# A value projection by seven quarter products per pair of blocks, with running sums kept in PSUM

## The chip, the cores and the metric

One core of one Trainium2 chip runs the kernel. The metric is the device time of one execution in microseconds; lower is better. The core's engines are TensorE (PE; its weight loads are shown apart as PEld), VectorE (DVE), ScalarE (ACT), GpSimd (POOL) and SyncE (SP), which here only issues DMAs. Matmuls write to PSUM, which has 8 banks of 128 x 512 f32; GpSimd's instructions here never touch it.

## What is computed

A transformer layer over 4096 rows of 512: attention with a window of 64, a residual and layer norm, then a gated feed-forward with int8 weights, a residual and layer norm.

```python
qkv = x @ w_qkv.T                      # 4096 x 512 by 512 x 1536, 16 heads of 32
q = q * cos + _rotate_half(q) * sin    # the same for k
scores = jnp.einsum('bhqd,bhkd->bhqk', q, k) * scale
keep = (rel >= 0) & (rel < window)     # window is 64
attn = jax.nn.softmax(jnp.where(keep[None, None], scores, -jnp.inf), axis=-1)
out = jnp.einsum('bhqk,bhkd->bhqd', attn, v) ... @ w_out.T
x = _layernorm(x + out)
gate = jax.nn.silu(_qmatmul(x, w_gate, s_gate))
up = _qmatmul(x, w_up, s_up)
x = _layernorm(x + _qmatmul(gate * up, w_down, s_down))
```

## The kernel before

The rows are cut into 8 tiles (0 to 7) of 512, a tile into 4 blocks of 128. One pass of the loop (`body`) does the attention of tile a and the feed-forward of tile f = a - 1. Each engine has its own instruction list, written out by hand; a `wait` stands before the instruction that needs it and holds up everything behind it on that engine. There is no scheduler.

On PE a pass runs: the value projection of a and its first score steps; 16 steps, each with one gate group (8 matmuls onto bank 0 or 2) and one up group (bank 1 or 3) of f, and between them the score steps and `weigh_v` (probabilities by values) of a; the output projection of a as two pairs (`project_o_pair`); the down projection of f; then q and k of tile a + 1 as two pairs (`project_pair`). A pair is two blocks, 2i and 2i + 1.

The projections of q and k and the output projection already used seven products for eight (Winograd's form): the input's four quarters (front, back block by low, high half of the 512 columns) and the weight's four quarters are combined into sums, and seven quarter products of two matmuls each give what eight would. Before, each product had a place of its own in PSUM and DVE added them up: `sum_second`, `sum_fourth`, `sum_back_odd` and four more for q and k, `sum_o_second` and eight more for the output. ACT copied only the first product (`keep_first`, `keep_o_first`). x's sums (`x_sums`) are made on DVE by `sum_x` (tile 1's second pair on POOL, by `sum_second_x`). The value projection was plain: `project_v`, four blocks of four 512-column matmuls, V0 at the end of the pass before, V1, V2, scores 0 and 1, V3. `keep_v` (ACT) rounded a block from its bank to f16 in `v_own`, and `split_v` (DVE) stored what rounding left.

After the q and k products: `rope_products` (DVE) reads the banks, `rope_sums` makes the rotated values in `fuse`, `split_high(j)` (ACT, four copies) and `split_low(j)` (POOL, four subtractions) split block j into two f16 parts, and SP transposes them (`turn_qk`, two DMAs a block, released by `qk_low`) into `qkT`. Blocks j and j + 2 share a buffer (`qk_split[j % 2]`), so `split_high(2)` and `split_high(3)` wait until the transposes of blocks 0 and 1 have landed (`wait_qkT`). In tile 0's pass SP issues half-size transposes (`first_turn_qk`).

Each tile's sums for the output projection overwrite columns 0 to 1023 of `wg` and 0 to 511 of `wu`; POOL loads them anew (`reload_columns`). In the first pass (`first`) PE projects q and k of tile 1, pair 1 last, ACT runs `split_x1_high(0..3)`, the split of the layer's middle rows, and DVE `split_x1`, `finish_x1`, then `rope_front(1)`.

## Time and profile before

| what | us |
| --- | --- |
| median of three runs (1166.36 to 1168.07) | 1166.68 |
| the profiled execution, first to last instruction | 1164.2 |
| PE busy | 1154.0 |
| DVE busy | 984.6 |
| ACT busy | 584.4 |
| POOL busy | 587.3 |

The profile is of one execution. An engine's busy time is no bound by itself; PE's share of the chain that ended last, and whether its groups follow each other without a hole, tell whether it bounds the kernel. The granted clock of PE is at its full level in all 40 slices but is shown only in tenths (9 is 90% or more). A 512-column f32 matmul stands as two entries in a timeline's count, so a quarter product of two matmuls is "x4". A row's duration includes the tail in which the next one already runs; distances between starts are what a group costs.

### The profile page before, as it was taken

The numbers are of one execution on the slowest core, as the hardware profiler recorded it, in microseconds if no ns is written. First come the engines' busy times: TensorE is split into PE (matmuls) and PEld (weight loads), VectorE is DVE, ScalarE is ACT, GpSimd is POOL, SyncE is SP. The second block draws the span as 40 slices with busy tenths as digits, with TensorE's granted clock in tenths as the row PEclk, the third lists the DMA queues.
The fourth block names the chain that finished last, engine by engine and source line by source line (L and its number), as shares of the span: only waits on it lengthen the run. The fifth ranks groups of instructions, "written<-read, shape, count | busy, mean of one in ns | idle before, by whom it ended". The sixth has DMA issues, their size and how long they took to land.

```text
span 1164.2 us, 25539 instructions
## 1 busy us (share of the span) xinstructions
PE 1154.0 (99%) x8433; PEld 567.9 (49%) x8433; DVE 984.6 (85%) x2821; ACT 584.4 (50%) x1640; POOL 587.3 (50%) x563
## 2 busy tenths in 40 slices
PE   9999999999999999999999999999999999999998
PEld 4344446444464444644455444554445444464444
DVE  7899998898987899879998899897898988986434
ACT  3953883048820588105880169701686027950330
POOL 0775684156731667326771367613676236752330
PEclk9999999999999999999999999999999999999999
DMA  9999786366562765617656096561964537734000
GB/s 295 173 175 252 137 166 160 66 88 137 111 149 55 110 131 107 145 41 128 132 97 141 37 146 119 101 132 46 155 123 88 131 63 137 120 73 109 19 2 36
DMA packets 352077, 134.80 MB, mean 116 GB/s; under 512 B 309840, under 2 KB 332496, under 8 KB 351952
## 3 DMA queue, kind: packets, MB, share of 16 engines
q1 hardware_dynamic: 334976, 106.86, 49.6%
q0 software_dynamic: 10560, 17.30, 5.1%
q10 hardware_dynamic: 6416, 9.00, 2.1%
q8 instruction: 75, 1.23, 0.5%
q14 instruction: 50, 0.41, 0.1%
HBM read 32.19 MB, written 8.39 MB: 35 GB/s over the span
## 4 chain that ended last, share of the span: by engine, by line
PE 97%; DVE 1%; ACT 1%; issue 1%; POOL 0%; POOLq 0%; DVEq 0%
PE bank L842 61%; PE bank L1058 18%; PE bank L848 10%; PE bank L984 3%; PE bank L964 2%; PE bank L864 1%; PE bank L1080 1%; ACT bank L1243 1%; PE bank L873 0%; PE bank L1069 0%; PE bank L948 0%; DVE wd L1373 0%; ACT wu L1186 0%; DVE ffn_tmp L1530 0%; ACT fuse L1186 0%
## 5 line engine op out<-in xcount | busy, mean ns | idle before, releaser
L842 PE MATMUL bank<-x1T,wg 128*128 128x512 f16 (+1 forms) x1032 | 242.5, 378 | 0.0
L842 PE MATMUL bank<-x1T,wu 128*128 128x512 f16 x1024 | 241.9, 379 | 0.0
L1243 ACT ACTIVATE bank<-bank,neg_max,qk_scale 128x128 f32<-128x128 f32 x512 | 220.5, 435 | 7.8 <-DVE neg_max L1558 6.1
L1058 PE MATMUL bank<-wd,fuse 128*128 128x512 f16 (+2 forms) x1056 | 222.7, 373 | 0.0
L660 POOL TENSOR_TENSOR fuse<-ffn_tmp,fuse 128x512 f16<-128x512 f32 x128 | 149.7, 1170 | 117.5 <-ACT fuse L1186 116.8
L742 POOL TENSOR_TENSOR fuse<-fuse 128x512 f16<-128x512 f32 x116 | 137.7, 1218 | 74.9 <-ACT fuse L1186 72.8
L1058 PEld LDWEIGHTS bank<-wd,fuse 128*128 128x128 f16 x1056 | 101.9, 98 | 118.0
L842 PEld LDWEIGHTS bank<-x1T,wu 128*128 128x128 f16 x1024 | 100.1, 98 | 120.7
L655 POOL TENSOR_TENSOR xT_sb<-probs,xT_sb 128x512 f16<-128x512 f32 x112 | 129.6, 1158 | 44.5 <-ACT xT_sb L1186 44.4
L842 PEld LDWEIGHTS bank<-x1T,wg 128*128 128x128 f16 x1032 | 96.3, 98 | 113.9 <-issue 4.0
L1196 ACT ACTIVATE ffn_tmp<-bank,tanh_scale 128x512 f32<-128x512 f32 x128 | 88.2, 689 | 100.0 <-PE bank L842 76.8
L848 PE MATMUL bank<-wqkv,xT_sb 128*128 128x512 f32 x296 | 133.6, 599 | 0.0
L1552 DVE CUSTOM_DVE_ANT_0 bank<-bank,mask_tile 128x128 f32<-128x128 f32 x448 | 116.3, 321 | 0.0
L1569 DVE SCALAR_TENSOR_TENSOR ffn_tmp<-bank,fuse_scale,ffn_tmp 128x512 f32<-128x512 f32 x128 | 96.1, 751 | 20.8 <-PE bank L842 9.9
L1565 DVE SCALAR_TENSOR_TENSOR ffn_tmp<-ffn_tmp,bank 128x512 f32<-128x512 f32 x128 | 86.9, 679 | 27.3 <-ACT ffn_tmp L1196 27.3
L1243 ACT ACTIVATION_READ_ACCUMULATOR bank<-bank,neg_max,qk_scale 128x1 f32 x512 | 107.0, 209 | 0.0
L823 POOL TENSOR_TENSOR rstd<-mean_var,half_power 128x1 f32<-128x1 f32 x32 | 23.8, 745 | 149.7 <-DVE mean_var L1586 144.2
L1186 ACT ACTIVATE fuse<-fuse 128x512 f16<-128x512 f32 x120 | 65.5, 618 | 55.0 <-DVE fuse L1381 54.5
L1530 DVE SCALAR_TENSOR_TENSOR probs<-bank,inv_sum 128x512 f32<-128x512 f32 x120 | 82.9, 691 | 4.8 <-DVE inv_sum L1525 0.3
L848 PEld LDWEIGHTS bank<-wqkv,xT_sb 128*128 128x128 f32 x296 | 54.7, 190 | 63.4 <-issue 61.7
L1186 ACT ACTIVATE fuse<-ffn_tmp 128x512 f16<-128x512 f32 x128 | 79.5, 621 | 8.2 <-DVE ffn_tmp L1569 8.2
L1373 DVE TENSOR_TENSOR fuse<-bank,tables 128x512 f32<-128x512 f32 x120 | 75.4, 680 | 1.5 <-ACT fuse L1186 1.0
(235 smaller groups left out, 1621.5 us busy)
## 6 DMA issues: line engine op xcount, KB each, us to landing
v_cross<-v_own SPq DMA_DIRECT2D x64, 128.0 KB, 2.4
out<-x ACTq DMA_DIRECT2D x31, 256.0 KB, 2.0
xT_sb<-xT SPq DMA_DIRECT2D x30, 256.0 KB, 4.1
qkT<-x SPq DMA_DIRECT2D x28, 256.0 KB, 3.8
wg<-w_gate POOLq DMA_DIRECT2D x7, 1024.0 KB, 5.2
wu<-w_up POOLq DMA_DIRECT2D x7, 512.0 KB, 6.0
wqkv<-w_qkvT SPq DMA_DIRECT2D x8, 256.0 KB, 6.3
wg<-w_gate POOLq DMA_DIRECT2D x1, 2048.0 KB, 8.4
```

The source lines that it names most:

```text
L655: done(probs_low, pool.tensor_tensor(place[:, 1, :, :], probs_place(s, ffn), place[:, 0, :, :], ALU.subtract))
L660: done(fuse_low, pool.tensor_tensor(fuse[:, s, 1, :], ffn_tmp[:, s % 2, :], fuse[:, s, 0, :], ALU.subtract))
L742: last = pool.tensor_tensor(*low_operands(j, i, ffn), ALU.subtract)
L842: last = pe.matmul(dst, lhsT, rhs, start=(i == 0), stop=(i == len(pairs) - 1))
L848: last = pe.matmul(dst, xT_sb[:, j, k, :], wqkv[:, k, cols], start=(k == 0), stop=(k == KC - 1))
L1058: last = pe.matmul(dst[:, cols], fuse[:, s, z, rows], wd[:, s, cols], start=(s == 0 and z == 0), stop=(s == STEPS - 1 and z == 1))
L1186: return act.activation(dst, src, ACT.Copy, scale=scale)
L1196: done(tanh_done, act.activation(ffn_tmp[:, s % 2, :], bank32[2 * (s % 2)], ACT.Tanh, scale=tanh_scale[:, s:s + 1]))
L1243: last = act.activation(unit, unit, ACT.Exp, bias=neg_max[:, s % 2, h // 3, h % 3:h % 3 + 1], scale=qk_scale[:, 2:3], accum_out=row_sum[:, ...
L1552: last = dve.tensor_tensor_reduce(out=unit, in0=unit, in1=mask_tile[:, :], scale=1.0, scalar=MASKED, op0=ALU.add, op1=ALU.max, accum_out=r ...
L1565: done(gated, dve.scalar_tensor_tensor(out=tmp, in0=tmp, scalar=1.0, in1=bank32[2 * (s % 2)], op0=ALU.add, op1=ALU.mult))
L1569: done(fused, dve.scalar_tensor_tensor(out=tmp, in0=bank32[2 * (s % 2) + 1], scalar=fuse_scale[:, s:s + 1], in1=tmp, op0=ALU.mult, op1=ALU ...
```

## The change

The value projection of tiles 1 to 7 becomes `project_values`: seven quarter products for each of the pairs 0 and 1, of two 256-column matmuls. The value weight's sums are made by POOL (`add_v_weights`, three per tile, and `lessen_v_weights` once) in the columns of `wu` above 1023, which POOL loads anew each tile, as those of `wg` (`reload_late_columns`, at step 2).

All three projections now keep running sums in PSUM. A product is added onto what the bank holds (`onto=True`), and where an intermediate sum is itself a result part, ACT first copies it to SBUF (`keep_fifth`, `keep_sixth`, `keep_seventh`, `keep_o_...`, `keep_values_...`), mostly to `late_rows`, the columns of `wg` above 1023 seen as f32. DVE adds two terms where it added up to four: three sums a pair for q and k, four row additions a pair for the output, one `add_v` a block for v. `keep_v` and `split_v` now read `late_rows` instead of a bank.

PE, value stage and its waits:

```diff
+            def quarter(dst, lhsT, rhs, onto=False):
+                return product(dst, [(lhsT[:, k, :], rhs[:, k, :]) for k in range(KC // 2)], onto)
...
+            def values_first(a, i):
+                front_low, front_high, back_low, back_high = x_quarters(i)
+                low_left, right_less_left, high_left, high_right = v_quarters()
+                wait(rope_read, pe, a, i)
+                done(v_product[i], quarter(v_places(i)[3], front_low, low_left))
+
+            def values_fifth(a, i):
+                low_left, right_less_left, high_left, high_right = v_quarters()
+                wait(x_summed, pe, a - 1, 7)
+                wait(v_weights_added, pe, a - 1, 2)
+                done(v_product[i], quarter(v_places(i)[1], x_sums(i)[:, 0, :, :], right_less_left))
...
+            def values_sixth(a, i):
+                wait(v_products_kept[i], pe, a - 1, 0)
+                done(v_product[i], quarter(v_places(i)[3], x_sums(i)[:, 1, :, :], added_v_weights(0), True))
...
+            def values_seventh(a, i):
+                wait(v_products_kept[i], pe, a - 1, 2)
+                done(v_product[i], quarter(v_places(i)[3], x_sums(i)[:, 2, :, :], added_v_weights(1), True))
...
+            def values_fourth(a, i):
+                front_low, front_high, back_low, back_high = x_quarters(i)
+                wait(v_products_kept[i], pe, a - 1, 3)
+                done(v_product[i], quarter(v_places(i)[2], back_high, added_v_weights(2)))
+
+            def project_values(a):
+                values_first(a, 0)
+                values_fifth(a, 0)
+                values_first(a, 1)
+                values_sixth(a, 0)
+                values_third(a, 0)
+                values_fifth(a, 1)
+                values_seventh(a, 0)
+                values_sixth(a, 1)
+                values_second(a, 0)
+                values_fourth(a, 0)
+                values_third(a, 1)
+                values_seventh(a, 1)
+                scores(a, 0, True)
+                scores(a, 1, True)
+                values_second(a, 1)
+                values_fourth(a, 1)
...
                     elif attn:
-                        wait(v_low, pe, a, 2 * s + 1)
+                        wait(v_added, pe, a - 1, 2 * s + 1)
```

PE, output projection of a pair (the third product is now the sixth):

```diff
+                done(o_product, quarter(chain, front_low, low_left))
                 wait(added, pe, a - 1, 1 - i)
-                if i == 0:
-                    wait(probs_ready, pe, a, STEPS - 1)
-                else:
-                    wait_o_sum(pe, a, 0, SUM_THIRD)
                 wait(out_weights_added, pe, a - 1, 3)
-                done(o_product, quarter(back_right, added_o(i, 2), added_out(2)))
-                wait(o_first_kept, pe, a - 1, i)
-                done(o_product, quarter(front_left, front_high, high_left))
+                done(o_product, quarter(other, added_o(i, 2), added_out(2)))
                 wait(added, pe, a - 1, 2)
-                if i:
-                    wait_o_sum(pe, a, 0, SUM_BACK_LEFT)
-                done(o_product, quarter(back_left, added_o(i, 1), added_out(1)))
-                done(o_product, quarter(front_right, added_o(i, 0), added_out(0)))
-                wait_o_sum(pe, a, i, SUM_SECOND)
-                done(o_product, quarter(back_left, back_high, added_out(3)))
+                wait(o_products_kept, pe, a - 1, 4 * i)
+                done(o_product, quarter(chain, added_o(i, 1), added_out(1), True))
+                wait(o_products_kept, pe, a - 1, 4 * i + 1)
```

ACT, in the loop and in the first pass:

```diff
+            def keep_values_first(a, i):
+                if i == 0:
+                    wait(pair_summed, act, a - 1, 3 * turn_of(1) + 2)
+                keep_value_product(a, i, late_rows(2 * i)[:, 0:HALF_EMB], v_places(i)[3], V_FIRST)
...
                 split_high(a + 1, 0, True)
+                keep_first(a + 1, 1)
                 for j in range(2):
                     split_x1_high(a, j, ffn)
                 split_high(a + 1, 1, True)
-                keep_first(a + 1, 1)
+                keep_fifth(a + 1, 1)
+                keep_sixth(a + 1, 1)
+                keep_seventh(a + 1, 1)
                 carry_v(a + 1)
...
+                    keep_values_first(a, 0)
+                    keep_values_fifth(a, 0)
+                    keep_values_first(a, 1)
+                    keep_values_sixth(a, 0)
+                    split_high(a, 2, ffn)
+                    keep_values_fifth(a, 1)
+                    keep_values_seventh(a, 0)
+                    keep_values_sixth(a, 1)
+                    split_high(a, 3, ffn)
                     keep_v(a, 0, ffn)
-                    split_high(a, 2, ffn)
                     keep_v(a, 1, ffn)
+                    keep_values_seventh(a, 1)
+                    exponentials(a, 0, ffn)
                     keep_v(a, 2, ffn)
-                    split_high(a, 3, ffn)
-                    exponentials(a, 0, ffn)
                     keep_v(a, NB - 1, ffn)
                     exponentials(a, 1, ffn)
...
+                    keep_seventh(a + 1, 0)
                     keep_first(a + 1, 1)
                     split_high(a + 1, 0, ffn)
+                    keep_fifth(a + 1, 1)
+                    keep_sixth(a + 1, 1)
+                    split_high(a + 1, 1, ffn)
+                    keep_seventh(a + 1, 1)
                     carry_v(a + 1)
```

DVE and POOL:

```diff
+            def add_v(a, j):
+                i, back = j // 2, j % 2
+                wait(v_products_kept[i], dve, a - 1, 2 + back)
+                wait(v_product[i], dve, a - 1, V_FOURTH if back else V_SECOND)
+                done(v_added, dve.scalar_tensor_tensor(out=late_rows(j), in0=bank32[j], scalar=v_scale[:, 1:2],
+                                                       in1=late_rows(j), op0=ALU.mult, op1=ALU.add))
...
+                    add_v(a, 0)
+                    add_v(a, 1)
                     for j in range(2):
                         split_v(a, j, ffn)
                     for s in range(2):
                         maxima(a, s, ffn)
                         bias(a, s)
+                    add_v(a, 2)
+                    add_v(a, 3)
+                    weights(a, 0, ffn)
                     split_v(a, 2, ffn)
-                    weights(a, 0, ffn)
                     split_v(a, NB - 1, ffn)
                     weights(a, 1, ffn)
...
             def rope_front(a, i):
-                sum_front_even(a, i)
-                wait(pair_summed, dve, a - 1, 7 * turn_of(i) + 4)
+                add_front_even(a, i)
+                wait(pair_summed, dve, a - 1, 3 * turn_of(i))
                 rope_products(a, 2 * i, True, range(2), paired=True)
-                sum_front_odd(a, i)
-                if i:
-                    sum_back_even(a, i)
-                wait(pair_summed, dve, a - 1, 7 * turn_of(i) + 5)
+                add_back_odd(a, i)
+                add_front_odd(a, i)
+                wait(pair_summed, dve, a - 1, 3 * turn_of(i) + 2)
                 rope_products(a, 2 * i, True, range(2, 4), paired=True)
                 rope_sums(a, 2 * i, True)
...
+                sum_first_x(0)
                 split_low(a + 1, 0, True, range(2))
                 invert_deviation1(a, 2)
                 split_low(a + 1, 0, True, range(2, 4))
+                lessen_v_weights()
+                add_v_weights(a + 1, None)
                 for j in range(2):
                     keep_x1(a, j, ffn)
...
+                    if s == 2:
+                        reload_late_columns(a, f, attn)
```

How the lists of instructions change at the three places that matter.

ACT at the head of the loop's pass, before. `v_own<-bank` is `keep_v`, the two rows `fuse<-fuse` together are `split_high` of one block (2, then 3), `bank,row_sum` are the exponentials:

```order
L1186 ACTIVATE v_own<-bank0,v_scale 128x16x32
L1186 ACTIVATE fuse<-fuse 128x16x2x16 x2
L1186 ACTIVATE fuse<-fuse 128x32x16 x2
L1186 ACTIVATE v_own<-bank1,v_scale 128x16x32
L1186 ACTIVATE v_own<-bank2,v_scale 128x16x32
L1186 ACTIVATE fuse<-fuse 128x16x2x16 x2
L1186 ACTIVATE fuse<-fuse 128x32x16 x2
L1243 ACTIVATE bank4,row_sum<-bank4,neg_max,qk_scale 128x128 x4
L1186 ACTIVATE v_own<-bank3,v_scale 128x16x32
```

The same place in the changed kernel; `wg<-bank` are the copies of value sums to `late_rows`:

```order
L1285 ACTIVATE wg<-bank1,v_scale 128x256
L1285 ACTIVATE fuse<-fuse 128x16x2x16 x2
L1285 ACTIVATE fuse<-fuse 128x32x16 x2
L1285 ACTIVATE wg<-bank2,v_scale 128x256
L1285 ACTIVATE wg<-bank1,v_scale 128x256
L1285 ACTIVATE wg<-bank3,v_scale 128x256
L1285 ACTIVATE fuse<-fuse 128x16x2x16 x2
L1285 ACTIVATE fuse<-fuse 128x32x16 x2
L1285 ACTIVATE v_own<-wg 128x16x32 x2
L1285 ACTIVATE wg<-bank3,v_scale 128x256
L1384 ACTIVATE bank4,row_sum<-bank4,neg_max,qk_scale 128x128 x4
```

Four copies now stand behind `split_high(2)`, and the last of them, of bank 3, also behind `split_high(3)` and two `keep_v`.

PE at the end of the value stage, before (V1, V2, scores 0 and 1, V3, first gate group):

```order
L848 MATMUL bank1<-wqkv,xT_sb 128x512 x4
L848 MATMUL bank2<-wqkv,xT_sb 128x512 x4
L964 MATMUL bank4<-qkT 32x96 x16
L964 MATMUL bank6<-qkT 32x96 x16
L848 MATMUL bank3<-wqkv,xT_sb 128x512 x4
L842 MATMUL bank0<-x1T,wg 128x512 x8
```

The same place in the changed kernel, from seventh(0) on:

```order
L876 MATMUL bank1<-wu,ffn_tmp 128x256 x2
L876 MATMUL bank3<-wu,probs 128x256 x2
L876 MATMUL bank0<-wqkv,xT_sb 128x256 x2
L876 MATMUL bank1<-wu,xT_sb 128x256 x2
L876 MATMUL bank2<-wqkv,probs 128x256 x2
L876 MATMUL bank3<-wu,probs 128x256 x2
L1063 MATMUL bank4<-qkT 32x96 x16
L1063 MATMUL bank6<-qkT 32x96 x16
L876 MATMUL bank2<-wqkv,xT_sb 128x256 x2
L876 MATMUL bank3<-wu,xT_sb 128x256 x2
L876 MATMUL bank0<-x1T,wg 128x512 x8
```

The last value product goes to bank 3, whose other half holds the sum that ACT must have copied.

ACT at the end of the first pass, before; `qkT<-x1` are the `split_x1_high`, `y<-bank4` the copy of the first product of pair 1, `v_cross<-v_cross` is `carry_v`:

```order
L1186 ACTIVATE qkT<-x1 128x512 x2
L1186 ACTIVATE fuse<-fuse 128x16x2x16 x2
L1186 ACTIVATE fuse<-fuse 128x32x16 x2
L1186 ACTIVATE y<-bank4 128x512
L1186 ACTIVATE v_cross<-v_cross,carry_scale 64x1024
L1186 ACTIVATE qkT<-x1 128x512 x2
```

And in the changed kernel:

```order
L1285 ACTIVATE qkT<-x1 128x512 x2
L1285 ACTIVATE fuse<-fuse 128x16x2x16 x2
L1285 ACTIVATE fuse<-fuse 128x32x16 x2
L1285 ACTIVATE wg<-bank7 128x512
L1285 ACTIVATE wg<-bank6 128x512 x2
L1285 ACTIVATE v_cross<-v_cross,carry_scale 64x1024
L1285 ACTIVATE qkT<-x1 128x512 x2
```

The last two `split_x1_high` now stand behind three copies of product sums.

## Rows read from the trace of the kernel before

**Rows 1.** Page: the span, and part 4, the chain by engine.
```profile
span 1164.2 us, 25539 instructions
...
PE 97%; DVE 1%; ACT 1%; issue 1%; POOL 0%; POOLq 0%; DVEq 0%
```

**Rows 2.** Timeline of PE, one tile: start us, us, engine, line, operation, names, count.
```profile
507.95 1.88 PE L842 MATMUL bank<-wqkv,xT_sb 128*128 128x512 f32 x4
...
531.98 10.46 PE L848 MATMUL bank<-wqkv,xT_sb 128*128 128x512 f32 x24
...
542.37 0.52 PE L964 MATMUL bank<-qkT 128*32 128x96 f16 x32
...
542.83 3.70 PE L848 MATMUL bank<-wqkv,xT_sb 128*128 128x512 f32 x8
...
546.36 1.89 PE L842 MATMUL bank<-x1T,wg 128*128 128x512 f16 x8
...
550.20 1.90 PE L842 MATMUL bank<-x1T,wg 128*128 128x512 f16 x8
```

**Rows 3.** Timeline of ACT, same tile; in brackets idle time before and releaser.
```profile
468.34 0.38 ACT L1186 ACTIVATE ffn_tmp<-bank 128x256 f32<-128x256 f32 x1 [0.20 <-PE bank L842]
...
522.37 2.18 ACT L1186 ACTIVATE fuse<-fuse 128x512 f16<-128x512 f32 x4
...
536.51 2.19 ACT L1186 ACTIVATE fuse<-fuse 128x512 f16<-128x512 f32 x4 [0.21 <-DMA qkT<-fuse]
```

**Rows 4.** Timeline of SP's DMA issues, and us to landing from the DMA view.
```profile
527.69 20.87 SPq L511 DMA_TRANSPOSE qkT<-fuse  x6
...
538.25 2.02 SPq L511 DMA_TRANSPOSE qkT<-fuse  x1
...
qkT<-fuse SPq DMA_TRANSPOSE x1, 4.3
...
24.59 11.94 SPq L521 DMA_TRANSPOSE qkT<-fuse  x8
...
35.19 1.34 SPq L521 DMA_TRANSPOSE qkT<-fuse  x1
...
qkT<-fuse SPq DMA_TRANSPOSE x1, 3.2
```

**Rows 5.** DVE and POOL, same tile; L1380 by source: ns min, median, max.
```profile
L1380 DVE TENSOR_TENSOR fuse<-fuse x29: 678/693/1455, 19.6 to 964.7; 128x512 f32<-128x512 f32 x29
...
539.97 1.64 DVE L1381 TENSOR_TENSOR fuse<-fuse 128x512 f32<-128x512 f32 x1
...
542.86 0.29 DVE L1552 CUSTOM_DVE_ANT_0 bank<-bank,mask_tile 128x128 f32<-128x128 f32 x1
...
545.43 0.74 DVE L1518 SCALAR_TENSOR_TENSOR v_own<-bank,v_scale,v_own 128x512 f16<-128x512 f32 x1
...
523.07 4.51 POOL L742 TENSOR_TENSOR fuse<-fuse 128x512 f16<-128x512 f32 x4 [4.74 <-ACT fuse L1186]
...
537.22 5.41 POOL L742 TENSOR_TENSOR fuse<-fuse 128x512 f16<-128x512 f32 x4 [1.98 <-ACT fuse L1186]
```

**Rows 6.** Timeline of PE and DVE in the output projection of pair 1.
```profile
475.80 1.03 PE L842 MATMUL bank<-wout,v_own 128*128 128x256 f32 x4
...
476.66 1.89 PE L842 MATMUL bank<-wg,x1T 128*128 128x256 f32 x8
...
476.02 0.42 DVE L1452 TENSOR_TENSOR x1T<-x1T,v_own 128x256 f32<-128x256 f32 x1
```

**Rows 7.** Timeline of tile 1: ACT, DVE, PE.
```profile
101.71 1.14 ACT L1186 ACTIVATE v_cross<-v_cross,carry_scale 64x1024 f16<-64x1024 f16 x1
...
102.75 0.62 ACT L1186 ACTIVATE qkT<-x 128x512 f16<-128x512 f32 x1
...
107.71 1.29 DVE L1373 TENSOR_TENSOR fuse<-bank,tables 128x512 f32<-128x512 f32 x2
...
120.59 1.89 PE L842 MATMUL bank<-x1T,wg 128*128 128x512 f16 x8
```

440 lines of the change are left out of this document (234 added, 206 removed).

## The prediction

> **What bounds the kernel now.** I read the page first, then the PE timeline of one tile in the middle of the loop, then what ACT, DVE, POOL and the DMA queue do beside it. The page puts 97% of the chain that ended last on PE [rows 1]. In the timeline the groups of matmuls start without a hole [rows 2], so every column that PE is spared is worth its time, and every wait put in front of PE costs its time. The tile that I use begins with the first product of pair 0 at 507.95; I call that T and count from it. The value projection starts at T+24.03 (531.98), is broken by the 32 matmuls of two score steps at T+34.42, and the first gate group starts at T+38.41 (546.36) [rows 2]. That is 14.38 us, of which the scores take 0.46 us, so the projection takes 13.92 us.
>
> **The saving.** A 256-column quarter product takes 0.86 us (475.80 to 476.66) [rows 6]. The new projection is 14 of them: 12.04 us. It spares 1.88 us a tile, 13.2 us over seven tiles. Without a new wait the execution of 1164.2 us would end near 1151. The rest of the text asks how much of this comes back as waits.
>
> **The value stage, tiles 2 to 7.** The order on PE is: first(0), fifth(0), first(1), sixth(0), third(0), fifth(1), seventh(0), sixth(1), second(0), fourth(0), third(1), seventh(1), scores, second(1), fourth(1). Products onto a running sum wait until ACT has copied the sum. A 256-column copy takes 0.38 us [rows 3], and there is always at least one other quarter, 0.86 us, in between, so copies alone would stall nobody. (A 512-column quarter of q and k takes 24.03 / 14 = 1.72 us [rows 2].) But ACT has split_high(2) and split_high(3) between them, 2.19 us each [rows 3], and these wait for the transposes of q and k of blocks 0 and 1, because two blocks share one buffer. fourth(1), PE's last value product, waits for the copy of seventh(1), which stands on ACT behind split_high(3) and behind two keep_v copies. Before, split_high(3) stood behind only what PE had already left. So the question is when block 1's transposes land.
>
> Upstream of it: split_high(0) starts at T+14.4 as before (522.37) [rows 3], because keep_first(1) waits for a product that ends at T+13.9 in both kernels. POOL's split_low(0) follows at T+15.1 and took 4.51 us alone, but 5.41 us beside DVE sums of two SBUF operands, which themselves then took up to 1.45 and 1.64 us, for a median of 0.69 [rows 5]. DVE now reaches rope_sums(1) some 5 us earlier, while split_low(0) runs, so I take 5.4: T+20.5 instead of T+19.7 (527.69, the first transpose) [rows 4]. split_high(1) now runs at about T+19.1, and split_low(1) is done at about T+25, so block 1's transposes stand right behind block 0's.
>
> Block 0's took 8.8 us (527.69 until ACT is let go at 536.51) [rows 3, 4]. What two blocks take back to back tile 0 shows: eight half transposes issued from 24.59, the last at 35.19, landing 3.2 us later [rows 4]; 13.8 us for both. (An issue alone takes 1.34 us there, so some of this may be SP's time and not the transfer's; full-size ones need half as many.) So block 1 lands at T+20.5+13.8 = T+34.3; with 19.7 it is T+33.5; if transposes overlap better than in tile 0, T+31 to T+32. Before, block 1's last transpose was issued at 538.25 and landed 4.3 us later, T+34.6 [rows 4]. It is issued 3 us earlier than before and lands hardly earlier, since the queue is what takes the time.
>
> From there: split_high(3) 2.1 (four copies pipelined), keep_v(0) and keep_v(1) 0.5 each, the copy 0.4, with semaphores 3.6 us. fourth(1) starts at T+37.9 and the first gate group at T+38.8, against T+38.4. PE would have wanted fourth(1) at T+24.0 + 13 x 0.86 + 0.5 = T+35.8. **The 1.88 us come back whole, and 0.4 on top.**
>
> **The second gate group.** It writes banks 2 and 3 and so waits for add_v(3). On DVE that stands behind split_v(0), split_v(1), the maxima and biases of steps 0 and 1 and add_v(2). PE comes to it 3.84 us after the first (546.36 to 550.20) [rows 2]. The maxima took 2.57 us for two steps (542.86 to 545.43) [rows 5]. split_v(0) can start 2.7 us after split_high(3) starts, at T+37.0. The two split_v now read two SBUF operands each while POOL runs split_low(3); by the lengthened sums [rows 5] I take 1.2 each (pipelined), 0.6 if they don't meet POOL. Then 37.0 + 2.4 + 2.6 + 1.4 = T+43.4 against T+42.6: 0.85 us of stall; with 0.6 each none. The Trainium skill ("SBUF — State Buffer", Who interferes with whom) says that a DVE instruction with two SBUF inputs contends with a GpSimd instruction that reads SBUF, and one with a single SBUF input does not. By that rule the new split_v pays what the sums paid, and the old one, whose first operand was in PSUM, did not; no row shows a split_v with both in SBUF.
>
> **The output projection, all seven tiles.** DVE goes from 18 instructions a tile to 8, ACT from two copies to eight. By the same slots (quarter 0.86, copy 0.38) each copy is there 0.2 to 0.3 us before PE wants it. One edge is new: the third product of pair 1 now is the sixth product and needs add_back_o(2). PE wants it where its third product started, 475.80; that sum started at 476.02 and ended at 476.44 [rows 6], and DVE comes to it about 0.35 us earlier than before. Cost 0.1 to 0.3 us less a small wait that goes; I take 0.15. The q and k pairs go from 7 DVE sums to 3 and from one ACT copy to four each; a slot is 1.72 us for a copy of about 0.6, and split_high(1), done at T+21.3, leaves the last copy (T+21.9) before its product (T+22.3). I find no stall; 0.4 us is the cover, and what passes it costs as much. (That DVE is the first to be late here if it slips: rope_done(1) lets split_high(1) go.) POOL's three weight sums, at split_low's 1.1 us or a little more each, fall into its idle time during the down projection; the reload of 2 MB of gate and up columns is issued at gate step 2 and needed at step 8, six steps of 3.5 us or more. Both at nothing, unless DMA contention counts (below).
>
> **Tile 1.** Here ACT's new order costs once. split_x1_high(2) ran at 102.75, then rope products of pair 1 started at 107.71 [rows 7]. Now split_x1_high(2) and (3) stand behind keep_seventh(1) and carry_v. PE's order up to there: second(1) early, first(1) at 92.9, project_o(3), then fifth, sixth, third, seventh, with about 0.4 us of waiting; seventh ends near 105.5. Copy 0.6, carry_v 1.14 [rows 7], so split_x1_high(2) ends at 107.8; split_x1(2), finish_x1(3), split_x1_high(3), split_x1(3) on DVE and ACT follow each other to 110.4, and pair 1's rope starts then, 3.4 us late. late_rows are free for the first value copy only after add_front_odd(1), near 114.1. PE wants sixth(0) at 107.9 + 2.6 = 110.5 and gets it at 114.5: 4 us. POOL's keep_x1(3) and split_low(1) also come 3.6 us later, block 1 lands near 121, rope_done(3) comes near 122, fourth(1) near 125.6, the first gate near 126.4 against 120.59 [rows 7]: 5.8 us lost. Bounds: 4 us (only the wait before sixth(0), less the 1.9 spared, plus the waits of the stage) to 7.
>
> **The sum.** Tiles 2 to 7: 0.4 + 0.85 + 0.15 = 1.4, six times 8.4. Tile 1: 5.8 + 0.85 + 0.15 = 6.8. Together +15 us: a span of 1179, and since the median of the runs lies 2.5 us above this execution's span, 1181.5 us. Bounds of the same story: no stall at the second gate and block 1 a little earlier (0.1 a tile) with 5 in tile 1 gives 1172; block 1 at T+35 and 7 in tile 1 gives 1187.
>
> **Rivals.** *Even in the loop.* Split_low(0) isn't lengthened, block 1 lands at T+33.5, no stall at the second gate: first gate at T+38.0, so -0.4 + 0.15 a tile, -1.5 in six; tile 1 +4.5: 1169.7. For it: part of tile 0's 13.8 us may be issuing, and DVE had slack before. 18%.
>
> *Faster.* Block 1's transposes land about 7 us after they are issued, whatever is before them, as block 1's last did within 4.3 us when the queue was empty: T+31 to T+32.2 [rows 4]. Then ACT reaches split_high(3) at T+31.9, the copy of seventh(1) is there at T+35.5 and PE never waits. The whole 1.88 less 0.15 holds: -10.4 in six tiles, +4 in tile 1: 1160.5. It decides at T+32.2: a landing before it brings all, each us after it costs one. Against it: eight half transposes took 13.8 us, not 9 [rows 4]. The Trainium skill ("Advanced Engine Details and Errata", X-Bar Transpose) expects 350 to 400 GB/s of transposes; a block is 1 MB, so by that page two blocks would take some 6 us and the rival would hold with room. The 13.8 us are 150 GB/s; here row and rule differ, and I go by the row. If tile 1 also recovered, 1155. 22%.
>
> *More stalls in the attention loop.* Everything after the second gate is 3 us nearer to PE: probabilities are split later on POOL, and the 2 MB reload is issued exactly when transposes of steps 2 and 3 run. If these land 1 to 2 us late, weigh_v waits 1 us a tile: 1189. 12%.
>
> *It doesn't do what it says:* 256-column products cost more than half of 512-column ones. The 0.86 us against 1.72 [rows 2, 6] speak against it; 1%, not priced.
>
> The forecast itself has the remaining 47%.
>
> **How the numbers follow.** A measurement of this kernel can tell about 0.2% (2.3 us) from no change. Faster: the faster rival, 22%. Same: half of the even rival, 9%. Slower: the rest, 69%. The range leaves out a tile 1 that recovers in the faster rival and the far end of the stalls: 1160 to 1189.
>
> **What would show it.** In the changed trace: the last value group of PE starts 37 to 38 us after T, with a hole of 1 to 2 us before it, let go by ACT wg; ACT's fuse copies before it are let go by DMA qkT. A hole of some 4 us at tile 1's fourth value product. The second gate group waits for DVE's wg. If instead the gate starts 36.7 us after T, the transposes were early and the faster rival holds. If the chain shows PE waiting at its half-bank copies in the output projection, my slots are wrong.

## The result: 1212.1 us, 3.9% slower

| | before | changed kernel |
|---|---|---|
| time, median of the runs | 1166.5 us (1166.2 to 1168.1) | 1212.1 us (1210.3 to 1213.7) |
| span of the profiled execution | 1164.2 us | 1208.9 us |
| mean granted clock of TensorE | 1.000 | 0.991 |

The ratio is 1.0386, with a 95% interval of 1.0367 to 1.0404. The forecast was 1181.5 us with a range of 1160 to 1189, so the time lies 23 us above the range's upper end.

The page of the changed kernel: its span, the chain that ended last by engine, and two of the DMA queues (packets, MB, share of 16 engines).

```profile
span 1208.9 us, 25954 instructions
...
q0 software_dynamic: 19008, 31.98, 9.3%
...
q8 instruction: 81, 1.33, 0.4%
...
PE 55%; issue 16%; POOL 11%; DVE 8%; DMA 6%; ACT 3%; SPq 1%; POOLq 0%; DVEq 0%; ACTq 0%
```

Before, PE had 97% of that chain and "issue" 1% [rows 1]. Now PE has 55%, and 16% is "issue", time in which an engine waited for nothing that the profile shows. PE no longer bounds the kernel by itself, but the 16% are not one cause: in the run below whose holes are gone they are still 13%, and in one with five such holes they are 2%. The stages tell more.

In PE's timeline I took the start of each stage and summed over the program; the last 33.4 us, from the last down projection on, are the same in both. The differences add up to the 44.7 us of span:

| stage | before | changed | difference |
|---|---|---|---|
| up to the first gate group of tile 1 | 120.6 | 129.5 | +8.9 |
| value stage, tiles 2 to 7 | 86.3 | 83.5 | -2.8 |
| feed-forward stages | 494.4 | 512.4 | +18.0 |
| output projection | 91.5 | 95.2 | +3.7 |
| down projection, all but the last | 193.7 | 193.7 | 0.0 |
| start of q and k to start of the value stage, tiles 2 to 7 | 144.2 | 161.1 | +16.9 |

**Of the 16.9 us, 16.5 are five holes of 3.2 to 3.4 us**, one at the start of the value stage of tiles 2 to 6 (measured from start to start; the idle time in a row's brackets is some 0.2 us less). Tile 7's value stage, and tile 1's, have none. Tiles 2 to 6 are those that TensorE reaches over a taken branch of its loop: the first pass and the last two are written out, and the loop is entered by falling into it. PE (first) and ACT around one of them, start us, us, engine, line, operation, names, count, and in brackets the idle time before and its releaser:

```profile
557.81 1.94 PE L876 MATMUL bank<-w_sums,xT_sb 128*128 128x512 f32 x4
562.82 2.07 PE L876 MATMUL bank<-wqkv,xT_sb 128*128 128x256 f32 x4 [3.06 <-issue]
564.68 1.62 PE L876 MATMUL bank<-wqkv,ffn_tmp 128*128 128x256 f32 x4
```
```profile
555.04 2.19 ACT L1285 ACTIVATE fuse<-fuse 128x512 f16<-128x512 f32 x4 [1.59 <-DVE fuse L1546]
557.14 0.57 ACT L1285 ACTIVATE wg<-bank 128x512 f32<-128x512 f32 x1
```

The row at 557.81 is `pair_fourth(1)`, the last product of the pass. It waits for the copy of the seventh product, ACT's row at 557.14, which ends at 557.71. The first product of the next pass starts 5.11 us after that; the same distance is 5.31, 5.27, 5.08 and 5.15 us in the other four passes. Only the 1.7 us of `pair_fourth(1)` lie over it.

**Behind the hole TensorE's clock falls.** The quarters at 562.82 and 564.68 take 1.86 and 1.46 us instead of 0.86. The windows of these stretches, with the busy time of each engine and then PEclk, DMA share and GB/s:

```profile
core 0: us, PE busy (x) PEld busy (x) DVE busy (x) ACT busy (x) POOL busy (x), PEclk, DMA share, GB/s
562.80:564.60 1.80, 1.78 (x4) 1.52 (x5) 1.76 (x4) 0.00 (x0) 0.00 (x0) 0.50 1.79 179
564.60:566.10 1.50, 1.50 (x5) 1.19 (x4) 1.22 (x2) 0.47 (x1) 0.00 (x0) 0.57 0.47 102
566.10:568.00 1.90, 1.90 (x10) 1.67 (x10) 0.00 (x0) 0.95 (x2) 0.00 (x0) 1.00 1.26 275
707.30:710.40 3.10, 0.15 (x1) 0.00 (x0) 3.06 (x6) 0.00 (x0) 1.35 (x2) 1.00 1.47 120
710.50:712.30 1.80, 1.80 (x8) 1.61 (x9) 1.77 (x4) 0.47 (x1) 0.00 (x0) 1.00 1.77 213
```

A granted clock of 0.50 is the lower of the two levels, 1.2 instead of 2.4 GHz. The last two rows are the next pass: a hole of 3.0 us, and no fall. Over the tiles the value stage takes 14.3, 14.5, 14.3, 12.8, 14.5 and 12.9 us, so four of the five holes brought the fall, at 1.5 to 1.7 us each. The clean stage, 12.84 us against 14.38 before, is the change's real saving, 1.54 us a tile.

**The feed-forward stages** lose 18.0 us, mostly in `weigh_v`, which waits for transposes of probabilities. PE at steps 0 to 3, and SP's issues of these transposes:

```profile
593.10 0.29 PE L1083 MATMUL bank<-xT_sb,v_cross 128*32 128x128 f16 x8 [0.69 <-DMA xT_sb<-xT_sb]
...
601.35 0.30 PE L1083 MATMUL bank<-y,v_cross 128*32 128x128 f16 x8 [0.49 <-DMA y<-xT_sb]
...
602.16 0.29 PE L1083 MATMUL bank<-y,v_cross 128*32 128x128 f16 x8 [0.40 <-DMA y<-xT_sb]
```
```profile
585.70 1.23 SPq L553 DMA_TRANSPOSE xT_sb<-xT_sb  x1
...
593.95 6.18 SPq L553 DMA_TRANSPOSE y<-xT_sb  x2
```

The first transpose is issued 8.6 us after the first gate group (577.15 to 585.70); before it was 5.5 us (546.36 to 551.82). In the DMA view the transposes to y take 6.0 us to land, against 3.1 before, in the stretch in which the 2 MB of late columns come in.

### The profile page after: what moved, and what is told of

Its sections match the earlier page's. It is cut to its first block, busy times and chain, and to the rows that moved or that the text cites. A ratio compares the mean times of both kernels' runs of the same rounds, so it can differ in the third digit from the quotient of the medians.

```text
span 1208.9 us, 25954 instructions
## 1 busy us (share of the span) xinstructions
PE 1159.1 (96%) x8601; PEld 606.4 (50%) x8601; DVE 977.0 (81%) x2727; ACT 641.1 (53%) x1777; POOL 645.0 (53%) x605
## 4 chain that ended last, share of the span: by engine, by line
PE 55%; issue 16%; POOL 11%; DVE 8%; DMA 6%; ACT 3%; SPq 1%; POOLq 0%; DVEq 0%; ACTq 0%
PE bank L876 34%; PE bank L1148 18%; POOL fuse L768 7%; DMA y<-xT_sb 4%; POOL xT_sb L656 2%; PE bank L1083 2%; ACT bank L1384 1%; DVE fuse L1538 1%; POOL fuse L661 1%; DVE qkT L1601 1%; PE bank L1063 1%; DMA out<-x 1%; DMA xT_sb<-xT 1%; ACT fuse L1285 1%; PE bank L902 1%
## 5 line engine op out<-in xcount | busy, mean ns | idle before, releaser
L768 POOL TENSOR_TENSOR fuse<-fuse 128x512 f16<-128x512 f32 x116 | 147.4, 1304 | 91.4 <-ACT fuse L1285 88.3
L656 POOL TENSOR_TENSOR xT_sb<-probs,xT_sb 128x512 f16<-128x512 f32 x112 | 129.9, 1160 | 79.4 <-ACT xT_sb L1285 79.2
L876 PEld LDWEIGHTS bank<-x1T,wu 128*128 128x128 f16 x1024 | 100.2, 98 | 120.6
L876 PE MATMUL bank<-wqkv,xT_sb 128*128 128x256 f32 (+1 forms) x216 | 84.1, 515 | 17.6 <-issue 15.7
L1285 ACT ACTIVATE fuse<-bank 128x512 f32<-128x512 f32 x24 | 14.3, 597 | 153.3 <-PE bank L876 153.3
L1285 ACT ACTIVATE wg<-bank 128x256 f32<-128x256 f32 (+1 forms) x84 | 37.9, 451 | 99.9 <-PE bank L876 99.9
```

Of the source, the lines that this page charges most:

```text
L656: done(probs_low, pool.tensor_tensor(place[:, 1, :, :], probs_place(s, ffn), place[:, 0, :, :], ALU.subtract))
L768: last = pool.tensor_tensor(*low_operands(j, i, ffn), ALU.subtract)
L876: last = pe.matmul(dst, lhsT, rhs, start=(i == 0 and not onto), stop=(i == len(pairs) - 1), skip_group_check=onto)
L1285: return act.activation(dst, src, ACT.Copy, scale=scale)
```

## Experiments on the loop's branch

In what follows theory A says that a taken branch of TensorE's loop costs a fixed way from the release of the last wait before it to the first product behind it, about 5 us, and that only work queued behind that wait covers it. Its rivals are an operand of the new products that comes late, and the longer program.

### Three quarters, or one, ahead of the branch

The comments behind `#` in the cuts of code are this text's.

```
-                values_first(a, 0)          # head of project_values(a), behind the branch
-                values_fifth(a, 0)
-                values_first(a, 1)
...
+                    values_first(a + 1, 0)  # behind the last project_pair, ahead of the branch
+                    values_fifth(a + 1, 0)
+                    values_first(a + 1, 1)
```

> The changed kernel, with one move: TensorE issues the first three quarter products of the value stage (first and fifth of blocks 0 and 1, first of blocks 2 and 3) at the end of a pass, ahead of the loop's branch, instead of behind it. Nothing is added or left out. Theory A (the hole of 3.0 to 3.3 us at the start of the value stage in passes 2 to 6 is TensorE's way over the loop's branch, about 5 us from the release of the last wait in the pass, of which only the 1.7 us of the last query/key product is covered): 2.6 us more of queued products lie over the branch, so the hole shrinks from 3.2 to about 0.7 us, the granted clock stays at 1.00 behind it, and each of five passes gets 2.5 + 1.4 = 3.9 us shorter: 1212 - 19.5 = about 1192 us. Theory B (the first value product waits for an operand or a bank: weight sums, row sums, the landing of rows): the hole stays 3.2 us long and now stands ahead of the branch, 1212 us within 3. Theory C (the end of the pass has to do with how many instructions the program has, not with what lies over the branch): the hole stays behind the branch, now at the sixth product, 3.2 us.

> As the run before it in this list, but with only the first quarter product (0.86 us) moved ahead of the branch. Theory A: the hole falls by just that, from 3.2 to 2.35 us (five passes: 1212 - 4.3 = 1208 us, less if the clock still halves behind it; 1200 if it does not). Theories B and C: no change of the hole, 1212 us.

Measured: 1209.0 us with three, 1208.8 us with one, a single run each. PE with three quarters ahead, then the windows behind the hole, then PE with one ahead:

```profile
263.08 1.03 PE L876 MATMUL bank<-wqkv,xT_sb 128*128 128x256 f32 x4
264.80 1.13 PE L876 MATMUL bank<-wu,ffn_tmp 128*128 128x256 f32 x4 [0.69 <-issue]
```
```profile
264.80:266.80 2.00, 2.00 (x9) 1.79 (x10) 1.97 (x4) 0.47 (x1) 0.00 (x0) 1.00 1.07 186
```
```profile
260.63 1.03 PE L876 MATMUL bank<-wqkv,xT_sb 128*128 128x256 f32 x4
264.14 1.79 PE L876 MATMUL bank<-wqkv,ffn_tmp 128*128 128x256 f32 x4 [2.48 <-issue]
```

The hole moves to whichever product is first behind the branch, and shrinks by what was queued: by the brackets 3.0 to 3.3, 2.3 to 2.5 and 0.5 to 0.7 us with none, one and three quarters ahead. From the end of the last copy to that product it is 5.1 to 5.4 us in all ten passes. No operand does this: the product that waited in one kernel starts at once in the other. So the hole is where theory A has it. The time is not as forecast with three quarters: three quarters should have given 20 us back, and 3 came. The value stages of tiles 2 to 6 now take 15.1 us on average, the 0.6 us hole among it, where 12.8 would be clean (products of blocks 2 and 3 wait 0.2 to 1.5 us for ACT's copies), and the feed-forward stages went from 512.4 to 522.1 us in sum: the second gate group waits 5.7 us in all for DVE instead of 1.2, and the waits let go by DMA went from 12.8 to 16.2 us. **The hole had hidden two other waits.**

### TensorE's passes written out

```
-            with eng.Fori(1, NT - 1) as t:
-                body(t, True, True, True)
+            if eng is pe_engine[0]:         # TensorE alone
+                for t in range(1, NT - 1):
+                    body(t, True, True, True)
+            else:
+                with eng.Fori(1, NT - 1) as t:
+                    body(t, True, True, True)
```

> The changed kernel with TensorE's six looped passes written out one after the other, so that TensorE takes no branch between passes; the other engines keep their loops. Same work, same order. Theory A: no hole at the start of any value stage (below 0.3 us), clock 1.00 there; but then what the hole had absorbed comes back before the last product of blocks 2 and 3, about 1 us a pass: 1212 - 5 x (4.6 - 1) = about 1194 us. Theory B: holes as before, 1212 us. Theory C (instruction volume): holes as before or more of them, 1212 us or above.

Measured: 1196.1 us. No value stage starts with a hole, and q and k take 24.1 us in every pass (24.0 before the change). Without a branch TensorE doesn't pay it, so 16 us are the branch's, net of what comes back. What comes back is what the prediction had named; PE and ACT in tile 2:

```profile
274.30 1.13 PE L882 MATMUL bank<-wqkv,xT_sb 128*128 128x256 f32 x4
276.74 1.13 PE L882 MATMUL bank<-wu,xT_sb 128*128 128x256 f32 x4 [1.30 <-ACT wg L1292]
...
282.14 1.04 PE L882 MATMUL bank<-x1T,wg 128*128 128x512 f16 x4 [0.53 <-DVE wg L1651]
```
```profile
273.09 2.19 ACT L1292 ACTIVATE fuse<-fuse 128x512 f16<-128x512 f32 x4 [2.12 <-DMA qkT<-fuse]
275.19 1.13 ACT L1292 ACTIVATE v_own<-wg 128x512 f16<-128x512 f32 x2
276.23 0.46 ACT L1292 ACTIVATE wg<-bank,v_scale 128x256 f32<-128x256 f32 x1
```

The last product waits for the copy at 276.23, which stands behind two `keep_v` copies, `split_high(3)` and the transposes that this waits for. That chain is the prediction's, link by link. It shows in three of the six tiles (1.30, 1.48 and 0.74 us) and not in the others; the second gate group waits 0.4 to 1.5 us for DVE's `add_v` in all seven tiles, 5.2 us in sum.

### The same hole in the kernel before

```
-                    project_v(a + 1, 0, ffn)        # end of the pass
...
+                    project_v(a, 0, ffn)            # behind the branch, ahead of project_v(a, 1, ffn)
```

In the first pass it is moved in the same way.

> The kernel before, in which the value projection of block 0 (3.43 us) is issued behind the loop's branch instead of ahead of it, so that the pass ends with the fourth product of the second pair, as it does in the changed kernel. No other edit. Theory A: a hole appears at the start of the value stage of passes 2 to 6 although the scheme is the old one; the last wait in the pass (for the fourth or third sum) lets go about 1.7 to 3.4 us of products, so the hole is 1.5 to 3.3 us, and 1166.5 + 5 x (1.5 to 4.7) = 1174 to 1190 us. Theories B and C (the hole comes from the new operands or the longer program): no hole, 1166.5 us within 1.

Measured: 1169.2 us, and no hole in any pass; the 3.0 us of span over the kernel before all stand ahead of tile 1's first gate group (123.6 instead of 120.6). My expectation was wrong, because I had not looked up which wait is the last. It is `wait(pair_summed, ..., 7 * turn + 1)`, ahead of the third product; it is released when the DVE row at 529.62 ends, at 530.30, and 4.63 us of work lie behind it (DVE, then PE):

```profile
529.62 0.68 DVE L1397 TENSOR_TENSOR ffn_tmp<-bank,ffn_tmp 128x512 f32<-128x512 f32 x1
```
```profile
533.22 1.88 PE L842 MATMUL bank<-w_sums,xT_sb 128*128 128x512 f32 x4
534.93 2.31 PE L848 MATMUL bank<-wqkv,xT_sb 128*128 128x512 f32 x5
```

So one more wait was added, for a sum that is ready 1.5 us before the product that waits for it:

```
                 done(qk_done, quarter(front_odd, sums[:, 3, :, :], high_odd))
+                wait(pair_summed, pe, a - 1, 7 * turn + 3)
                 done(qk_done, quarter(back_even, back_high, w_sums[:, 2, :, :]))
```

> The run with the kernel before whose value projection of block 0 stands behind the loop's branch, and one wait more: the fourth product of the second pair, the last one of the pass, waits for VectorE's fourth running sum of that pair (event 7 x turn + 3), which ended at 531.76 us in that run, 1.5 us before the product's turn. So the wait costs nothing where it stands; it only keeps TensorE's sequencer from running ahead. In the run without it the last wait was for the second sum (530.30), 4.6 us before the next pass, and there was no hole. Theory A (TensorE's first product behind a taken branch comes 5.1 us after the release of the last wait before it): a hole of 531.76 + 5.1 - 534.93 = 1.9 us at the start of the value stage of passes 2 to 6, though nothing of the scheme is changed; 1169.2 + 5 x 1.9 = 1178.7 us, and up to 5 x 1.6 more if the clock halves behind it. Rival (the hole belongs to the new products' operands, or to the longer program): no hole, 1169.2 us.

Measured: 1188.5 us, 19 us more for one wait that is met in time in every pass. DVE, PE and windows:

```profile
541.36 0.70 DVE L1407 TENSOR_TENSOR bank<-bank,ffn_tmp 128x512 f32<-128x512 f32 x1
```
```profile
543.52 1.88 PE L842 MATMUL bank<-w_sums,xT_sb 128*128 128x512 f32 x4
547.67 10.56 PE L848 MATMUL bank<-wqkv,xT_sb 128*128 128x512 f32 x24 [2.27 <-issue]
```
```profile
255.50:257.50 2.00, 2.00 (x3) 0.91 (x4) 1.97 (x3) 0.00 (x0) 0.95 (x1) 0.64 0.40 92
257.50:259.50 2.00, 2.00 (x4) 0.77 (x3) 2.00 (x5) 0.00 (x0) 0.00 (x0) 0.51 1.07 171
```

Five holes of 2.3 to 2.4 us stand at the start of the value stage, and in three of the five passes the value stage takes 16.2 instead of 14.4 us, with the clock as in the windows. 5 x 2.35 + 3 x 1.8 = 17 of the 19 us; the other 2 stand ahead of tile 1's first gate group (125.7 instead of 123.6). From the sum's end to the first product it is 5.5 to 5.6 us here. With the old scheme, the old operands and the old program length the hole is there: theory A holds, and both rivals fall. One thing stays open: 4.63 us were enough in the run without the added wait, 5.1 to 5.6 were needed in the others. The way over the branch is therefore not one constant.

**The trace tells more of that way.** Among its DMA packets are those that bring the engines their instructions ("instruction": q8, whose total the page above has, and q14). The DMA view of the changed kernel from 560.2 to 560.4 us, and of this run from 545.1 to 545.2, both inside a hole (packets, MB, share of 16 engines):

```profile
q8 instruction: 1, 0.02, 29.2%
```
```profile
q8 instruction: 1, 0.02, 58.4%
```

Each is one packet of 16 KB that takes 0.93 or 0.94 us, and the first product behind the hole starts 2.50 and 2.51 us after it does. All 20 holes of the four kernels with such holes have this packet on q8, 2.46 to 2.70 us ahead of the product. With TensorE's passes written out, and the other engines' loops kept, q8 moves nothing in the 9 us ahead of the value stages of tiles 2 to 6. So the branch most likely makes TensorE wait for a load of instructions; that is argued from the times, since the profile doesn't say which engine a queue serves. What differs between the runs is the way from the last release to the packet, 2.6 to 3.1 us in the 20 passes; where 4.63 us were enough, a packet starts 1.1 to 1.2 us after the release (much the same in tile 7's written-out pass, so it needn't be the branch's). What sets that part stays open.

### The branch somewhere else

TensorE's loop is cut between the down projection's second and third block, as VectorE's already is in a like manner; and VectorE's maxima go first, as in the run of the next section.

```
+            def front(t, more, attn=True):   # values, feed-forward, output projection, down(0), down(1)
+            def back(t, more, attn=True):    # down(2), down(3), project_pair(a + 1, 0), (a + 1, 1)
-            bodies(pe, first, body)
+            halved_bodies(pe, first, front, back, last_body)
```

> The changed kernel with TensorE's loop kept, but its branch moved to a place with queued work behind the last wait: a looped pass now runs from the second half of the down projection to the first half of the next one (VectorE's loop is already cut in such a way), so a down block of 32 products, 6.9 us, lies over the branch. VectorE's maxima of slots 0 and 1 go first, as in the earlier run with passes written out (1191.1 us). Theory A: no hole at the start of any value stage and the clock at 1.00 there, 1191 us within 2, that is 21 us below the changed kernel with the same arithmetic. If a branch costs a hole wherever it stands (rival), five holes of 3 us stand in the down projection: about 1206 us.

Measured: 1200.5 us (1196.6 to 1201.9), ratio to before 1.028 [1.026, 1.030]. The value stages have no hole of that kind, but the down projection takes 28.8 to 28.9 us instead of 27.7 in the four passes with the branch in it, and the holes are there:

```profile
370.32 2.54 PE L1148 MATMUL bank<-wd,fuse 128*128 128x512 f16 x11 [0.27 <-issue]
373.51 11.61 PE L1148 MATMUL bank<-wd,fuse 128*128 128x512 f16 x53 [0.64 <-issue]
```

The first product behind the branch (370.32) waits 0.3 us here and under 0.15 in the other three passes; the twelfth waits 0.6 to 0.9, and again a 16 KB packet on q8 starts 2.4 to 2.6 us ahead of it. Both sides had a part of the truth: the branch moves its cost with it, and with more queued work over it that is 1.1 to 1.3 us a pass instead of 3.3. The time is 9 us above that with the passes written out and the maxima first, and 8.2 by the two profiled spans: 4.6 in the down projections, 2.7 in the value stages, 2.4 up to tile 1's first gate group, 0.3 in the output projections, and -1.8 in the feed-forward. Why the middle two differ, one profiled execution of each can't say (the four runs of this kernel spread over 5 us, those of before over 2).

## Experiments on the rest

### VectorE's order at the start of the feed-forward

Before, DVE took the maxima of slot 0 at 542.86, 3.5 us ahead of the first gate group [rows 5]. In the changed kernel it makes the low parts of value blocks 0 and 1 first and comes to the maxima 0.3 us ahead of it (577.15):

```profile
574.62 2.27 DVE L1650 TENSOR_TENSOR v_own<-wg,v_own 128x512 f16<-128x512 f32 x2 [0.62 <-ACT v_own L1285]
576.82 0.29 DVE L1687 CUSTOM_DVE_ANT_0 bank<-bank,mask_tile 128x128 f32<-128x128 f32 x1
```

```
-                    for j in range(2):
-                        split_v(a, j, ffn)
                     for s in range(2):
                         maxima(a, s, ffn)
                         bias(a, s)
+                    for j in range(2):
+                        split_v(a, j, ffn)
```

> The changed kernel with TensorE's passes written out (the earlier run of that kind: 1196.1 us), and VectorE takes the maxima of score slots 0 and 1 ahead of the low parts of value blocks 0 and 1, which it now makes first (2.3 us, after a wait for ScalarE's high parts). Theory D (the first wait of the attention loop, 0.5 to 1.5 us a pass at the weighting of slot 0 for the transposes of its probabilities, comes from the softmax of slot 0 being 3 us later against the feed-forward's start than before): the first probability transposes start about 2 us earlier, that wait goes, 7 passes x 0.5 to 1.3: 1187 to 1192.5 us. Rival E (those waits come from the 2 MB reload, whatever the softmax does): the waits stay, 1196 us within 1.

Measured: 1191.1 us against 1196.1, one run each. The variants that were run four times spread over 3 to 8 us, so the 5 us by themselves show little; the waits of the two traces do. The first transpose of probabilities of tile 2 is issued 7.9 instead of 9.3 us after the first gate group, and yet the waits let go by DMA stay: 9.8 us in sum over the seven tiles without this order, 10.8 with it. What went is the wait of the second gate group for DVE's `add_v(3)`, from 5.2 to 0.5 us in sum. VectorE used to stand still for ScalarE's high part of block 0 ahead of the maxima, and `add_v(3)` stood behind both; now the maxima fill that time. PE at the place of the row at 282.14 above:

```profile
279.22 0.35 PE L1069 MATMUL bank<-qkT 128*32 128x96 f16 x16
279.51 1.90 PE L882 MATMUL bank<-x1T,wg 128*128 128x512 f16 x8
```

So theory D isn't borne out: the softmax of slot 0 does come later, but with it taken 1.4 us earlier those waits are what they were.

### Where the 2 MB reload stands

```
-                    if s == 2:
+                    if s == 4:
                         reload_late_columns(a, f, attn)
```

> TensorE's passes written out, and GpSimd issues the 2 MB reload of the late gate and up columns at step 4 of the feed-forward instead of step 2 (about 8 us later). Theory E (the second pair of waits of the attention loop, 1.0 to 1.4 and 0.4 to 0.6 us before the weighting of slots 2 and 3, whose transposes to y take 6.2 us for two while 2 MB go through the same queues): these two waits fall to below 0.3 us; unless the same appears at a later slot, 7 x 1.5: about 1186 us. If the gate products of step 8 wait for the later reload, that shows before them, and the sum is 1196 or above. Rival D (late softmax alone): waits unchanged.

Measured: 1213.2 us, 17 us slower than with the reload at step 2. The waits for slots 2 and 3 went, as theory E has it, and greater ones came at slots 4 and 5; all waits let go by DMA are 22.5 us in sum, against 9.8:

```profile
314.25 0.30 PE L1089 MATMUL bank<-xT_sb,v_cross 128*32 128x128 f16 x8 [2.38 <-DMA xT_sb<-xT_sb]
...
315.93 0.40 PE L1089 MATMUL bank<-xT_sb,v_cross 128*32 128x128 f16 x8 [1.27 <-DMA xT_sb<-xT_sb]
```
```profile
304.90 6.75 SPq L559 DMA_TRANSPOSE xT_sb<-xT_sb  x2
```

> As the second run of this list, with the 2 MB reload issued at step 1 of the feed-forward instead of step 2, about 4 us earlier. Moving it 8 us later cost 17 us, since the waits went to slots 4 and 5 and grew. Theory E (the reload delays whichever transposes it meets): the waits before slots 2 and 3 shrink, at the price of one before slots 0 and 1; -5 to +3 us against the run before: 1182 to 1190 us. A draw would say that the reload's place doesn't matter as long as it is early.

Measured (the edit is the same with `s == 1`): 1237.4 us, ratio 1.060 [1.058, 1.061]; 38 us slower than the run with the seventh copy first, described below (1199.0 us), from which it differs by this line alone. One wait a tile, at slot 1, is now

```profile
302.27 0.41 PE L1083 MATMUL bank<-xT_sb,v_cross 128*32 128x128 f16 x8 [5.64 <-DMA xT_sb<-xT_sb]
```

The reload was issued from 291.92 on, and the transpose of slot 1 at 294.75. Of the 36 us that the feed-forward stages are longer, 29 are such waits; behind this one the clock falls too (0.50 from 302 to 307 us). My forecast of -5 to +3 us was far off: I had priced the wait by those of slots 2 and 3 and not by what the transfer takes (6.7 and 8.5 us for its halves, by the DMA view).

Then the same bytes from the same step on, in four DMAs of 512 KB at steps 2 to 5, with a reference that is measured as often:

```
-                    if s == 2:
-                        reload_late_columns(a, f, attn)
+                    if 2 <= s < 6:
+                        reload_late_columns(a, f, attn, s - 2)   # two of w_gate, then two of w_up
```

> The changed kernel with TensorE's passes written out, VectorE's maxima of slots 0 and 1 first and ScalarE's copy of the seventh value product ahead of the high parts of value blocks 0 and 1. Expected from the two earlier runs, 1191.1 us with written-out passes and maxima first, and a looped pair in which the copy's place was worth 1.5 us: 1189 us, 1186 to 1193, still 20 us above the kernel before. Left in the trace: no hole behind a branch, 4.1 us in tile 1, and 1.5 to 2.5 us a pass before the weighting of slots 2 and 3.

> As the run before it in this list, with the 2 MB reload cut into four DMAs of 512 KB, issued at steps 2, 3, 4 and 5. Theory E (the transposes of slots 2 and 3 are late because they share the DMA engines with 2 MB that are in flight at once): each meets at most 512 KB, the waits before slots 2 and 3 shrink from 1.2 and 0.5 us to below 0.5 together, nothing larger comes back at slots 4 and 5, and the time falls by 5 to 8 us, to 1181 to 1184 us. Rival (any reload between transposes costs a change-over each time, whatever its size, as a later start cost 17 us and an earlier one 38 us): it gets slower, by 5 us or more, 1194 us or above.

Measured: 1190.7 us (1187.2 to 1195.2), ratio 1.021 [1.018, 1.024], in one piece; 1183.3 us (1179.9 to 1188.0), ratio 1.015 [1.012, 1.018], in four. The two sets of four runs just overlap, but the stages agree with the medians: the feed-forward stages fall from 511.9 to 504.8 us in sum, 7.1 of the 7.5 us between the profiled spans, and the waits let go by DMA fall from 9.4 to 4.6 us. In tile 4 the waits for slots 2 and 3 are gone, and that for slot 5 is small:

```profile
590.11 0.30 PE L1091 MATMUL bank<-xT_sb,v_cross 128*32 128x128 f16 x8 [0.36 <-DMA xT_sb<-xT_sb]
```

So the reload meeting the transposes was worth 7 us here, and the rival, a cost for each change-over, falls. The feed-forward stages are still 10.4 us above those of before; a kernel without the reload at all wasn't tried, since the rows that it brings back are overwritten by the running sums.

### The copy of the seventh product first

```
+                    keep_values_seventh(a, 1)
                     keep_v(a, 0, ffn)
                     keep_v(a, 1, ffn)
-                    keep_values_seventh(a, 1)
```

> As the run before it in this list, and ScalarE copies the seventh value product of blocks 2 and 3 ahead of the high parts of value blocks 0 and 1 (2 x 0.55 us) instead of behind them. Theory G (as the prediction had it: the last value product waits for this copy, which stands behind the splitting of block 3 and these two): in the passes in which it waited, 0.7 to 1.5 us, 1.1 us goes: 3 to 4 us less in all, 1187 us. The high parts come 0.5 us later, and with them the low parts on VectorE; if the weighting of slot 0 then waits for the latter, it is a draw, 1191 us.

Measured: 1199.0 us (1196.3 to 1202.6) against 1200.5, inside the spread of the runs. The value stages of tiles 2 to 7 sum to 80.5 us with the edit and 84.1 without, and to 77.9 against 81.5 in the pair with passes written out (the run with the reload in one piece, and the one with the maxima first). So the copy's place costs 0.6 us a tile in this stage, as theory G has it; but the feed-forward stages took 517.9 against 509.2 us in the two profiled executions, and it comes back there.

### Tile 1

The hole of tile 1, as its rows in the changed kernel show it, has the size that was predicted and the chain too, 3 us later than forecast; PE, then ACT:

```profile
117.58 1.13 PE L876 MATMUL bank<-wu,ffn_tmp 128*128 128x256 f32 x4 [3.93 <-ACT wg L1285]
```
```profile
111.79 0.63 ACT L1285 ACTIVATE qkT<-x 128x512 f16<-128x512 f32 x1 [1.22 <-DVE x L1735]
117.06 1.20 ACT L1285 ACTIVATE wg<-bank,v_scale 128x256 f32<-128x256 f32 x3 [4.63 <-DVE bank L1567]
```

In the first pass VectorE's order was changed:

```
-                split_x1(a, 2, ffn)
                 finish_x1(a, 3, ffn)
-                split_x1(a, 3, ffn)
                 rope_front(a + 1, 1)
+                split_x1(a, 2, ffn)
+                split_x1(a, 3, ffn)
                 rope_back(a + 1, 1)
```

> TensorE's passes written out, and in the first pass only VectorE's order is changed: rows of block 3 are finished and the sums and rotations of the second pair made ahead of the low halves of rows 2 and 3. Theory F (the 4.1 us hole of tile 1 at the sixth value product: the copy of the first product waits until VectorE has read the kept products of the second pair, at 116.9 us, since these lie where the value products go): that reading ends near 113, the hole falls from 4.1 to about 0.5 us, the clock stays at 1.00 behind it (about 2 us): 1196.1 - 5 = 1191 us, if the row transposes of blocks 2 and 3 are not then late for the first gate products. Rival, as the prediction had it (ScalarE's queue order, the copies behind the row splits): the hole stays above 3 us.

Measured: 1197.4 us, 1.3 more than without the edit, which is no difference between single runs. The hole fell to 0.32 us, as theory F has it, and a longer one opened 16 us later:

```profile
114.12 1.13 PE L882 MATMUL bank<-wu,ffn_tmp 128*128 128x256 f32 x4 [0.32 <-ACT wg L1292]
130.29 2.07 PE L882 MATMUL bank<-wu,xT_sb 128*128 128x256 f32 x4 [6.61 <-ACT wg L1292]
```

The last value product now waits for ACT's splitting of block 3, which the trace shows idle for 7.10 us for DMA qkT. The end of tile 1's value stage is set by that chain of transposes; the first hole only hid a part of it.

## Why the prediction was wrong, step by step

**The step that failed** is the one on the q and k pairs: "I find no stall; 0.4 us is the cover". The slot sum was right as far as it went. The last copy is there before its product, if by 0.1 us and not 0.4 (557.71, 557.81), and no product of a pair waits. What it left out is what stands behind that product: the pass's end. Before, the last wait for a sum stood ahead of the third product, and block 0's value projection lay behind it too: 4.6 + 3.4 us of work over the branch. The change puts a wait ahead of the very last product and moves the value projection behind the branch. Priced by the runs, that is 3.2 to 3.4 us a pass, and the fall of the clock in four of five, about 23 us in all: the five holes' 16.5 and 4 x 1.6. The trace of before held no row for it, since nothing was ever uncovered there; its only sign was the position of the wait in the code. The Trainium skill ("Advanced Engine Details and Errata", Control Flow Timing) gives some 51 ns for a branch and 108 ns for one with a compare; here 5.1 to 5.6 us pass from the last release to the first product behind the branch, which such figures don't explain, and the trace decides.

**The saving** was put at 1.88 us a tile and is 1.54 (12.84 us from 710.49 to 723.33, against 14.38). The quarter is 0.86 us as read from [rows 6], but the one behind the hole, the one ahead of the scores and the one behind them take 0.95 to 0.97 until the next.

**fourth(1)** was to wait 2.1 us a tile (T+37.9 against T+35.8), and the first gate group to come 2.3 us late. In the changed kernel it waits in none of the tiles 2 to 7: the hole at the branch gives the transposes 3.3 us more. With the hole gone it waits as described, 1.30 us in tile 2, but only in half of the tiles. The mechanism was right and the size too great, by a factor of 4 with its zeros. The term that was mis-sized is the landing of block 1: with the passes written out ACT is let go at T+32.5 to T+34.0 in the six tiles, for a forecast of T+34.3, and each us counts above some T+32.2, as the faster rival had it. The 150 GB/s taken from tile 0's half-size transposes don't hold for full-size ones: those of the kernel before move at some 290 GB/s once they run (531.2 to 534.2).

**The second gate group** (0.85 us) waits 0.68 us in tile 1 and 0.47 in tile 7 and not between, for the same reason; 0.4 to 1.5 us with passes written out. Its premise that a `split_v` with two SBUF operands is slowed by POOL is borne out; L1650 by source, ns min, median, max:

```profile
L1650 DVE TENSOR_TENSOR v_own<-wg,v_own x28: 680/689/1646, 127.6 to 1019.3; 128x512 f16<-128x512 f32 x28
```

The one of block 1 takes 1.64 us in all seven tiles, with POOL busy throughout, and those of blocks 2 and 3, with POOL idle, 0.68. The one of block 0 takes 0.7 us in six tiles though POOL is busy too. The old one, with an operand in PSUM, took 0.74 beside POOL [rows 5].

**The output projection** (0.15 us a tile) has its wait where it was said, at the sixth product of pair 1 for `add_back_o(2)`, and it is 0.4 us:

```profile
503.39 1.13 PE L876 MATMUL bank<-wg,x1T 128*128 128x256 f32 x4 [0.41 <-DVE x1T L1593]
```

The stage is 0.5 us longer in each of seven tiles, +3.7 us instead of +1.1.

**Tile 1** (6.8 us) cost 8.9 us up to its first gate group and 4.7 in its feed-forward. The hole is 3.93 us for a forecast of 4; it wasn't said that the clock falls behind it (0.50 and 0.71 in the windows 119 to 121 and 121 to 123 us), which makes the stage some 1.7 us longer (18.6 = 12.8 + 4.1 + 1.7). By luck the stage is as long as forecast (18.5, from 107.9 to 126.4): the forecast had block 1's late landing in it, and the run has the clock's fall. What is late is its start, 110.90: ahead of it PE waits 1.89 us at 94.41 for DVE's x and 0.69 us at 109.08 for ACT's copy, where the forecast had 0.4 us in all.

**The attention loop.** The forecast put it at nothing and gave a rival with 1 us a tile 12%. The stages cost 18.0 us more over seven tiles; of the waits that the trace names in them, 12.8 us are let go by DMA (9.6 of these by the two transposes to y that the reload meets), and 1.2 by DVE's `add_v`. The rival named two causes. The reload is confirmed by moving and cutting it. The late softmax is not: taken 1.4 us earlier, it left these waits as they were. A single wait of 0.5 us in tile 7 is for DVE's `probs`. Some 3.5 us of the 18.0 stand in no wait that the trace names, and stay unexplained.

From the forecast's +15 to the measured +44.7 us the terms moved so: the branch and its clock +23, not in the sum at all; the feed-forward stages 18 instead of 6 (the second gate group's), +12; tile 1's value stage 8.9 instead of 5.8, +3; the output projection +2.6; and the value stages of tiles 2 to 7, without the clock's part, -9.2 instead of +2.4, so -12. The best version that the runs led to (passes written out, maxima and seventh copy first, reload in pieces) is still 1.5% slower than the kernel before: its stages spare 9 us in the value projection and lose 10 in the feed-forward, 10 up to tile 1's first gate group and 3 in the output projections.

## What to carry to other kernels

Before moving a wait or a block of work across the end of a loop's pass, look up the last wait of each engine ahead of its branch and sum the work queued behind it; on TensorE here 5 us were needed, and a wait that is always met in time cost 19 us by standing there. When a hole of one cause is removed, look for the waits that it hid: removing some 20 us of holes at the branch gave back 3 us, or 16, by what stood behind them. A reload is priced by the transfers that it meets, not by its own deadline.

## What the runs showed of the hardware

- From the release of TensorE's last wait in a looped pass to its first product behind the branch 5.1 to 5.6 us passed (20 passes of four kernels); 4.63 us of covering work were enough in a fifth. In all 20 a 16 KB instruction packet started 2.5 to 2.7 us ahead of that product.
- The granted clock fell to 0.50 (1.2 GHz) behind holes of 2.3 to 3.4 us in 10 of 15 looped passes, and not in the other five, one of them with a hole of 3.0 us; behind holes of 0.6 us it stayed at 1.00. The fall cost 1.5 to 1.8 us each time.
- A transposing DMA that took 3.1 us to land took 6.0 beside 2 MB of plain reload, and one issued 2.8 us after that reload kept PE waiting 5.6 us; in pieces of 512 KB on four steps the same bytes cost 7 us less in the whole program.
- A DVE tensor_tensor with both operands in SBUF (128x512) took 1.64 us beside a busy POOL and 0.68 beside an idle one, though 0.7 us in six of seven tiles at the block before, where POOL was busy too.
